# The first tile's keys picked on TensorE, and the start of a cross-attention and mixture-of-experts layer reordered

## What is computed

```python
# x (4, 512, 256), ctx_1024 (4, 1601, 256), seg ids (4, 512) in 0..127
x = x + tanh(g_xattn) * xattn(layernorm(x), ctx, seg)
x = x + tanh(g_ffn) * moe(layernorm(x))

# xattn: 16 heads of 16; each token sees 4 context rows
q = h @ Wq.T;  k, v = split(ctx @ Wkv.T)
rows = seg[:, :, None] - arange(4)      # below 0: masked
scores = q . k[rows] / 4;  o = softmax(scores) . v[rows];  out = o @ Wo.T

# moe: softmax of 8 gate logits, the best 2 kept
out = sum_e comb[e] * (silu(h @ w1[e] + b1[e]) @ w2[e] + b2[e])
```

## Time and profile before

| | us |
|---|---|
| median of 3 runs | 354.44 (353.26 to 354.62) |
| the profiled execution | 353.07 |
| its span, first to last instruction | 351.2 |

### The profile page before, as it was taken

The page is one execution under the profiler, slowest core; times in us unless marked ns, Lnnn a source line. Parts: engine busy times, 40 slices in busy tenths (PEclk is TensorE's granted clock), DMA queues, the critical chain, the costliest instruction groups (busy, mean ns, idle before and its releaser), DMA issues.

```text
span 351.2 us, 11438 instructions
## 1 busy us (share of the span) xinstructions
PE 322.4 (92%) x3486; PEld 265.9 (76%) x3486; DVE 268.2 (76%) x629; ACT 174.2 (50%) x490; POOL 207.7 (59%) x227
## 2 busy tenths in 40 slices
PE   8698999999898799999999999999999999999930
PEld 7467888888797687888888888888888887778710
DVE  4769999999998867878787788877887785665520
ACT  2452455555466267465656555565656633243400
POOL 3486889996762250748557576576574774662330
PEclk9999999999999999999999999999999999999995
DMA  7799999998999420233223323133232423231210
GB/s 245 244 350 417 405 418 401 417 401 331 360 381 379 141 65 19 37 60 47 48 37 60 63 34 63 33 63 55 41 47 49 63 36 59 39 66 23 35 20 12
DMA packets 31422, 53.23 MB, mean 152 GB/s; under 512 B 4850, under 2 KB 25570, under 8 KB 29316
## 3 DMA queue, kind: packets, MB, share of 16 engines
q0 software_dynamic: 9408, 26.63, 29.7%
q1 hardware_dynamic: 16628, 22.46, 17.8%
q10 hardware_dynamic: 5328, 3.37, 3.1%
HBM read 42.29 MB, written 10.17 MB: 149 GB/s over the span
## 4 chain that ended last, share of the span: by engine, by line
PE 67%; DVE 20%; issue 4%; POOL 2%; ACT 2%; DMA 1%; ACTq 0%; POOLq 0%; DVEq 0%
PE ps L1134 29%; PE ps L1148 16%; PE ps L1151 8%; DVE ps L1317 5%; PE ps L1162 2%; DVE sel L1313 2%; PE ps L1156 2%; DVE w_parts L1313 2%; PE ps L911 2%; DVE xs L1349 1%; PE ps L1155 1%; PE ps L1150 1%; PE ps L970 1%; DVE rden L1336 1%; PE ps L883 1%
## 5 line engine op out<-in xcount | busy, mean ns | idle before, releaser
L1134 PE MATMUL ps<-sel,w_parts 128*128 128x128 f16 x1776 | 141.7, 219 | 1.0 <-issue 0.8
L1134 PEld LDWEIGHTS ps<-sel,w_parts 128*128 x1776 | 119.4, 98 | 26.3 <-issue 1.8
L862 ACT ACTIVATE sel<-ps,b1T 128x128 f32<-128x128 f32 x296 | 84.3, 368 | 90.4 <-PE ps L1134 89.2
L627 POOL DMA_INDIRECT out<-sel x37 | 63.2, 1709 | 84.3 <-DVE sel L1599 69.8
L1148 PE MATMUL ps<-w_parts,sel 128*128 x259 | 96.4, 379 | 0.4
L1151 PE MATMUL ps<-w_parts,sel 128*128 x259 | 70.6, 273 | 0.0
L1554 DVE SCALAR_TENSOR_TENSOR sel<-sel 128x512 f16<-128x512 f32 x74 | 51.3, 693 | 2.5
L619 POOL DMA_INDIRECT sel<-tokens_split,sel x37 | 43.4, 1174 | 15.9 <-DVE sel L1522 9.3
L1540 DVE SCALAR_TENSOR_TENSOR w_parts<-w_parts (+1 forms) x32 | 39.0, 1220 | 10.0 <-issue 5.9
L614 POOL TENSOR_TENSOR sel<-sel 128x1 f32<-128x1 f32 x37 | 40.4, 1091 | 2.9 <-PE ps L1162 2.8
L1552 DVE TENSOR_SCALAR sel<-sel 128x512 f16<-128x512 f32 x74 | 33.1, 447 | 9.9 <-ACT sel L862 9.6
(11 more groups left out here) (230 smaller groups left out, 462.9 us busy)
## 6 DMA issues: line engine op xcount, KB each, us to landing
w_parts<-in_L_ffn_w SPq DMA_DIRECT2D x16, 1024.0 KB
out<-xs SPq DMA_DIRECT2D x16, 128.0 KB
tokens_split<-xsplit ACTq DMA_DIRECT2D x13, 128.0 KB
xs<-in_x ACTq DMA_DIRECT2D x2, 512.0 KB, 7.9
xs<-in_x SPq DMA_DIRECT2D x2, 512.0 KB, 7.2
near_rows<-w_parts SPq DMA_DIRECT2D x4, 256.0 KB, 6.1
sel<-tokens_split,sel POOLq DMA_INDIRECT x37
out<-sel POOLq DMA_INDIRECT x37
```

The source lines that it names most:

```text
L627: pool.indirect_dma_start(out_rows, bass.IndirectOffsetOnAxis(slot_row[:, at(q - 1)], 0), y_sb[(k + 3) % 4], None, compute_op=ALU.add).the ...
L862: act.activation(h32[n][:, c * P:c * P + P], ps_h[n][:, c * P:c * P + P], ACT.Silu, bias=biases[:, c:c + 1], scale=1.0 / (X_SCALE * W_SCALE))\
L1134: mm = pe.matmul(ps_h[n][:, c * P:c * P + P], w, xx, start=(i == 0), stop=(i == len(products) - 1))
```

## The change

- The segment ids of tile 0 are broadcast to all partitions. GpSimd makes four one-hot matrices from them, and TensorE multiplies these with the keys of batch 0 (`picks`), which gives the keys of tile 0's windows. ScalarE copies them to `picked`. Tile 0's values still come by its gather.
- Wkv is turned and copied in halves, the key half first. Batch 0's keys and values are two products of 256 columns with two copies; so `kv_ok` counts to 5. The copy of the value half stands behind first_x(0).
- Tile 0 of x is loaded by itself; tiles 4 to 7 come over SP's queue; tiles 12 to 15 are issued once batch 0's write has landed. The small inputs move from ACT's queue to SP's.
- GpSimd's first norms come in four calls: tile 0, tiles 1 to 3, 4 to 7 (between gathers 1 and 2), 8 to 15 (in step 1, behind gathers 3 and 4). VectorE's for tiles 8 to 15 go into its step 0.
- Batch 1's and 2's keys and values are computed behind query(1) and ahead of query(2), batch 3's in step 2, the turns of the gate weights and of b1 in step 3; the b2 work moves to step 2 on GpSimd.
- Most of the warm-up matmuls in the first stage are removed or cut; ScalarE loads its table earlier.

```diff
@@ SP @@
+            sp.dma_start(near_seg, seg_tiles[0:1, :].to_broadcast([P, P])).then_inc(s["near_in"], 16)
...
+            def near_out(b):
+                sp.wait_ge(s["kv_ok"], b + 2)
                 sp.dma_start(kv_near[b], kv_sb[:, b, :]).then_inc(s[f"kv_out{b}"], 16)
-                if b == 0:
-                    tokens_in(3)
+
+            near_out(0)
+            sp.wait_ge(s["kv_out0"], 16)
+            tokens_in(3)
+            near_out(1)
...
+                if t in (1, 3):
+                    near_out(2 + t // 2)
@@ GpSimd @@
-            first_norms(1, slice(0, TPB))
...
+            pool.wait_ge(s["near_in"], 16)
+            pool.tensor_copy(near_win, near_seg).then_inc(s["near_f"], 1)
+            pool.wait_ge(s["near_f"], 1)
+            pool.tensor_scalar(near_win, near_win, float(1 - WIN), 0.0, ALU.add, ALU.max).then_inc(s["near_w"], 1)
...
+            for j in range(WIN):
+                pool.tensor_scalar(pick_hot[:, j, :], near_win, float(P - WIN), away[:, j:j + 1], ALU.min, ALU.is_equal)\
+                    .then_inc(s["hot_ok"], 1)
+            first_norms(1, slice(0, 1))
+            first_norms(2, slice(1, TPB))
...
-            gather(0, TPB)
-            first_norms(2, slice(TPB, T))
...
+            with pool.If(general < 1):
+                pool.wait_ge(s["pick_ok"], 2)
+                pool.sem_inc(s["sel_k"], 1)
+                pool.wait_ge(s["kv_out0"], 16)
+                pool.indirect_dma_start(slot(0).rearrange("p j c -> p (j c)"), None, kv_near[0],
+                                        bass.IndirectOffsetOnAxis(win_near[:, 0:1], 0)).then_inc(s["sel_in0"], 16)
...
+            gather(1, 2)
+            first_norms(3, slice(TPB, 2 * TPB))
+            gather(2, 3)
             for t in range(T - 1):
                 if t >= 1:
                     values(t - 1)
                 if t >= 4 and t % 2 == 0:
                     norms(t - 4, 2)
-                if 0 < t < 3:
-                    gather(t + 3, t + 4)
+                if t == 1:
+                    gather(3, 5)
+                    first_norms(4, slice(2 * TPB, T))
+                elif t == 2:
+                    gather(5, 6)
...
@@ ScalarE @@
+            keys_or_values(0)
...
+            first_x(0)
+            keys_or_values(1)
...
-            first_x(0)
             act.wait_ge(s["wT_ps"], 1)
...
             first_turned(0)
+            for h in range(2):
+                act.wait_ge(s["pick_ps"], h + 1)
+                act.activation(picked[:, 512 * h:512 * h + 512], ps[:, 2 + h, :], ACT.Copy).then_inc(s["pick_ok"], 1)
             first_x(1)
...
+            first_x(2)
+            exponentials(0)
             keys_values(1)
...
-            for t in range(T - 1):
+            for t in range(1, T - 1):
...
+                if t == 2:
+                    keys_values(3)
+                if t == 3:
+                    small_turned()
@@ TensorE @@
+            def picks(h):
+                pe.wait_ge(s["kv_ok"], 1)
+                pe.wait_ge(s["hot_ok"], 2 * h + 2)
+                for j in (2 * h, 2 * h + 1):
+                    mm = pe.matmul(ps[:, 2 + h, j % 2 * D:j % 2 * D + D], pick_hot[:, j, :], kv_sb[:, 0, 0:D],
+                                   start=True, stop=True)
+                mm.then_inc(s["pick_ps"], 1)
...
             first_turn(0)
+            picks(0)
+            picks(1)
             query(0)
...
+            first_turn(1)
+            query(1)
             keys_values(1)
...
+            weight_turn(wo_raw, 7)
+            first_turn(2)
             pe.wait_ge(s["wT_ok"], 2)
...
+            keys_values(2)
+            query(2)
+            pe.wait_ge(s["kv_ok"], 4)
...
             for t in range(1, T - 1):
-                if t == 1:
-                    spin(20, 4)
-                query(t + 1)
-                if t == 1:
-                    spin(20, 4)
+                if t > 1:
+                    query(t + 1)
                 values(t - 1)
...
                 outputs(t - 1)
+                if t == 2:
+                    keys_values(3)
+                if t == 3:
+                    small_turn()
@@ VectorE @@
+            for b in range(2):
                 dve.wait_ge(s[f"x_in{b}"], 16)
...
+                if t == 0:
+                    dve.wait_ge(s["x_in2"], 16)
+                    first_norm(2 * TPB, 3 * TPB)
                 if added:
                     residual(t - 2)
...
+                if t == 0:
+                    dve.wait_ge(s["x_in3"], 16)
+                    first_norm(3 * TPB, T)
```

More of the change, by code:

```diff
@@ L300, in slot, with keys_of, norm_group @@
                 .rearrange("p (j c) -> p j c", j=WIN)
+        def keys_of(u):
+            return slot(u)[:, :, 0:D] if u else picked.rearrange("p (j c) -> p j c", j=WIN)
+        def norm_group(u):
+            return 1 if u < 1 else 2 if u < TPB else 3 if u < 2 * TPB else 4
         def tiles_in(t, *lags):
@@ L665, in keys_values @@
             def keys_values(b):
-                act.wait_ge(s["kv_ps"], b + 1)
+                act.wait_ge(s["kv_ps"], b + 2)
                 act.activation(kv_sb[:, b, :], kv_bank[b], ACT.Copy).then_inc(s["kv_ok"], 1)
-            keys_values(0)
-            def first_x(u):
-                act.wait_ge(s["shift1_ok"], 1 if u < TPB else 2)
-                wait(act, "xnT_ps", u - 1)
-                act.activation(xn[:, u % 2, :], xs[:, u, :], ACT.Identity, scale=rstd1[:, u:u + 1],
-                               bias=shift1[:, u:u + 1]).then_inc(s["xn_ok"], 1)
             def first_turned(u):
@@ L912, in keys_values @@
                 mm.then_inc(s["kv_ps"], 1)
-            for n in range(2):
-                pe.wait_ge(s[f"wkvT_ok{n}"], 1)
-            keys_values(0)
+            pe.wait_ge(s["ctxT_ok"], 1)
+            pe.wait_ge(s["wkvT_ok1"], 1)
+            for h in range(2):
+                pe.wait_ge(s["wkvT_ok0"], h + 1)
+                for c in range(KC):
+                    mm = pe.matmul(kv_halves[h], ctxT[:, 0, c, :], WkvT[:, c, D * h:D * h + D],
+                                   start=(c == 0), stop=(c == KC - 1))
+                mm.then_inc(s["kv_ps"], 1)
             general = flag(pe)
@@ L1279, in _, with first_norm @@
             v.tensor_scalar(win_f[:, :], segt[:, :], float(1 - WIN), 0.0, ALU.add, ALU.max).then_inc(s["segt_ok"], 1)
+            def first_norm(first, last):
+                for t in range(first, last):
+                    v.bn_stats(st1[:, t, :], xs[:, t, :]).then_inc(s["stats1"], 1)
+                for t in range(first, last):
+                    dve.wait_ge(s["stats1"], t + 1)
+                    v.bn_aggr(mv1[:, t, :], st1[:, t, :]).then_inc(s["aggr1"], 1)
+            dve.wait_ge(s["x_first"], 16)
+            first_norm(0, 1)
+            dve.wait_ge(s["wkvT_ps"], 1)
+            v.tensor_copy(WkvT[:, 1, 0:D], ps[:, 3, 0:D]).then_inc(s["wkvT_ok1"], 1)
             dve.wait_ge(s["segt_ok"], 2)
```

187 lines of the change are left out of this document (112 added, 75 removed).

## The result

| | before | after |
|---|---|---|
| median, same chip | 354.53 (353.26 to 354.97, 4 runs) | 359.39 (358.44 to 359.77, 4 runs) |
| profiled execution | 353.07 | 359.07 |
| its span | 351.2 | 357.4 |
| score product of tile 0 starts | 20.28 | 18.72 |
| of tile 1 | 24.86 | 28.82 |

The ratio is 1.0139, with a 95% interval of 1.0105 to 1.0173: the change costs 4.9 us by the medians, 6.0 by the two profiled executions. Behind tile 5 nothing changed: the span less the start of tile 5's product is 307.8 before and 308.0 after.

What follows compares the result with a forecast made beforehand. Bound by VectorE's attention steps, so the start of tile 5's product counts. Tile 0 -4.2, given back at tile 1 (+4.7), then +4.5 at tile 4: +5.0, giving 358.1 profiled, 359.4 median; range 354.0 to 362.5.

Steps and rivals of the forecast that it cites:

- First tile: Start of tile 0's score product: 16.1 instead of 20.28, through picked keys, a gain of 4.2 us.
- The "nothing" for the 40 warm-up matmuls: TensorE before values(0): removing the 40 warm-up matmuls, 2.6 us, was priced at nothing.
- the one-hots late: Rival at GpSimd's start: through only at 12.5, tile 0's product at 18, everything another 1 to 2 us later; no separate chance.
- First wait: Tile 1's product waits for its gather, landing at 25.2: start 25.3 against 24.86, +0.5 instead of -4.2.
- Second wait: Batch 1's write holds gather 4, values(1), keys_values(3), exponentials(3): tile 4's product at 43.7, +5.0; +3 to +5.9, chance 0.38.
- The marks: Signs for the second wait: gather 4 after 28 behind near_rows, values(1) after 32.
- Clock falls too: TensorE idle from about 29 to 36, then half clock, 2 to 3 us more: +7.4, 361.8; chance 0.20.
- Burst: Batch 1's write lands about 2 behind gather 1, at 27.2, all behind it 2.8 earlier: +2.1, 356.5; chance 0.17.
- The packet rule: DMA queues from 24.1 to 27.4 before the change: the write's packets went in turn with the gather's, 137 beside 147.
- Faster: Keys' head start kept: gather 0 starts at 14.7, tile 1's product at 23.1, write by 25: -2.0, 352.4; chance 0.12.
- no second wait: Batch 1's write lands by 25.5, values(1) starts at 29.7, only tile 1's +0.5 is left: 354.9; chance 0.13.
- The rest: Other parts hidden or nothing; gathers 3 to 7 have 1.7 us and more in hand once steps are 5 us late.

Runs made afterwards that it cites:

- the kernels with gather 0 at 17.06 and 15.31: Changed kernel with gather 0 not waiting for picked keys: 360.00; that plus VectorE one-hots, ScalarE-issued batch 0 write, earlier picks, batch 1's keys behind query(0): 357.43.
- the last kernel: Against the swapped-gathers kernel without extra warm-ups: last x quarter issued once batch 0's values are computed, gather 2 before first_norms(3), residual(0) behind step 2's softmax; 355.48, ratio 1.0034.
- the four kernels that ran on the first chip: Against the changed kernel: gather 0 freed, 360.00; norms of eight tiles behind values(1), 360.01; both, 358.12; 50 matmuls keeping the clock up ahead of the picks, 357.87.
- two pairs: Changed kernel with gather 0 freed plus norms of eight tiles behind values(1), ratio 1.0146; or plus batch 1's keys and values ahead of first_turn(0), ratio 1.0105.

## Why the prediction was right, and where it was not

The median was forecast at 359.4 and is 359.39; the profiled execution at 358.1 and is 359.07. The sum, +5.0, came out as +5.97 in the pair of traces. It hit through two terms that were off in opposite directions.

- **First tile.** Forecast 16.1, measured 18.72. The segment row landed at 7.55, not 6.9; GpSimd's 128x128 operations took 0.7 instead of 0.55, so scale and shift came at 13.2, not 11.9; the picks took 3.3 instead of 2.1. The bound of 1.0 for a one-hot would have held the time; the value taken was too near the low end. The picks were priced at full clock, though TensorE's last work ahead of them ended at 10.19 and the turn of tile 0 started at 13.97. This is the step that failed: the sum has no term for the clock behind that wait. With the wait filled the picks took 1.89. The "nothing" for the 40 warm-up matmuls is another matter: they stood ahead of values(0), not ahead of the picks. The rival "the one-hots late" had K0 at 18.
- **First wait.** Forecast +0.5, measured +3.96. The distance from gather 0's start to gather 1's landing, 9.4, was right (9.55), and so was the rule that gather 0 waits for the picked keys. The whole error is the start, 19.17 for 15.8. In the changed kernel the x load took nothing from it: it landed at 19.94, and gather 0 needed 5.65 us. But freeing the start alone gains little, since the interval grows (11.0 and 12.4 in the kernels with gather 0 at 17.06 and 15.31). For those the move of the x load behind batch 0's write, priced at 0 to +0.5, is what it turns on: with it undone in the last kernel, tile 1 landed 5.8 behind the start of its gather, not 8.8.
- **Gather 2.** It has no term in the prediction. Issued at 24.18 behind the first norms of tiles 4 to 7 (before: 17.49), it landed at 34.01, and tile 2's product waited 0.97 us for it: +1.06 of the 5.97.
- **Second wait.** The marks were met: write landed at 29.87 (30.0), gather 4 at 30.13 (30.3), values(1) at 33.76 (34.2), its 1.76 us of waiting named as near_rows. The landing was hit by luck: it was put 4.8 us behind that of gather 1, forecast at 25.2; gather 1 landed at 28.72 and the write 1.15 behind it. In the four kernels that ran on the first chip it was 1.2 to 3.7. From values(1) to K4 it took 10.85 where 9.5 was forecast, and 9.46 in three other traces, where values(1) ran at full clock on TensorE, the changed kernel's second one among them. It added only 0.94 to the sum, since VectorE was by then late anyway. That the chain is there with a price of its own is shown by the kernel with gather 0 freed, where VectorE would have been ready for K4 at 41.9 (K3 + 4.76) and it came at 46.43, and by its pair with the norms moved, where it came at 42.13. The kernel with the gathers swapped (ready at 42.1, K4 at 44.89) shows the end of the chain, but there gather 0 led to it and not the write alone.
- **Clock falls too.** It fell twice, at waits of 3.78 and 3.06 us. The second time TensorE's last matmul had ended at 29.61, and the granted clock was 0.80 from 31 to 32 us: sooner than the 4.4 us that the rival took from the earlier trace rows. The price forecast for it, 2 to 3 us, is near what the picks (1.5) and the way to K4 (1.4) cost; the first of these was at a place that the rival did not look at. The Trainium skill, "TensorE: Matmul & The Clock Gate" (HAM oscillation), describes this fall in waits for a DMA; the traces here agree for waits on ScalarE's copies, with a granted clock of 0.70 from 15 to 20 us.
- **Burst.** Its time, 356.5, did not come, but the write went much as it says. These are the DMA queues of 23.8 to 27.4 us, where SP's has no packet although the write was issued at 23.54, and then of 24.8 to 28.8, where it has 155 (the first weights among them), all behind 27.4:

```profile
q0 software_dynamic: 126, 0.90, 94.4%
...
q0 software_dynamic: 127, 0.91, 64.1%
q1 hardware_dynamic: 155, 0.34, 21.4%
```

So the write did not go in turn with the gathers for 4.8 us as in the earlier trace rows; it waited, and landed 1.15 behind gather 1, where the rival had about 2. It came late because gather 1 did. The write took 6.3 us from issue to landing, where batch 0's took 2.0. The packet rule of the Trainium skill, "DMA: Bandwidth & Descriptors" (Queues, rings and completion order), that an engine drains a whole packet from one ring before it switches, is not refuted by the earlier trace rows as the prediction has it: the rows count packets of all engines together and do not show in what order one engine took them.

- **Faster, no second wait.** Neither. Even with nearly everything mended the kernel is 0.34% behind.
- **The rest.** Gathers 3 to 7 were costed at nothing because the steps are late. That is so in the changed kernel (K3 without a wait) and stops being so as soon as the steps are early: 1.60 us in the last kernel. Steps of 4.76 us from tile 5 on: as forecast.

So the number was right. Both waits are there, in the places named. But the first was underpriced by 3.5 us, gather 2 had no term, and the write's landing was right by two errors that cancel; the sum held because two waits side by side cost only the longer. The median's exactness is partly luck, as the two profiled executions differ by 6.0 and the medians by 4.9.

## What to carry to other kernels

The picked keys let VectorE start 1.6 us sooner, and it then waited for a transfer that the same edit had made later: before moving a load behind something, read what the DMA engines do in the stretch it leaves. Here that stretch fell from 88% to 46% busy, and once the first gather was early the moved load ran beside it: 8.8 us to the landing, 5.8 with the load moved back. And when two chains end at the same place, expect nothing from mending one: none of the single repairs made this kernel measurably faster, and two pairs came to ratios of 1.0146 and 1.0105 against 1.0161.

## What the runs showed of the hardware

- Matmuls whose results nobody reads can be part of the timing: behind a wait of 3.78 us the granted clock is at half and eight 128x256 float matmuls take 3.32 to 3.62 us; with fifty matmuls of ones in that wait it stays full and they take 1.89. Warm-up matmuls that end 5.1 us ahead of the work did nothing (clock 0.71 against 0.65).
- A comparison of 128x128 floats takes 0.70 us on GpSimd and 0.22 on VectorE, more than three times as long, where the prediction scaled from a product of two tensors.
- The same first gather took 5.6 us from its start to its landing (before and changed; tile 1's in the last kernel 5.8), and 7.1 to 9.1 in six kernels where the x load had been issued 0.3 to 0.8 us ahead of it (with gather 0 freed 7.14, with the gathers swapped 7.58).
- A 256 KB write on SP's queue took 6.3 us to land when two gathers had been issued ahead of it (changed) and 9.6 behind four (before); batch 0's, with no gather beside it, took 2.0 and 2.6.
- The first loads land with a spread of 1.2 us between executions (the segment row at 7.32 to 8.48), and all of the start moves with them; a shift of under 1 us between two traces of this kernel means little by itself.
